# Rotary embedding of two cross attentions: a product on TensorE against elementwise work over two feature chunks

## The chip, the cores and the metric

One core of one Trainium2 chip runs the whole program. The metric is the device time of one execution in microseconds, the median of several runs.

## The reference, cut to what matters

The program is a decoder of two layers over 8 sequences of 512 tokens with 256 features. Each layer has a self attention, a cross attention and a feed-forward part. The change touches the two cross attentions. Both have 16 heads of 16 features, take queries from the normalised stream and keys and values from `ctx_1024` (8 x 512 x 256), and rotate pairs of features of queries and keys by an angle that depends on the token:

```python
# first cross attention: neighbouring features are a pair
x1, x2 = x[..., ::2], x[..., 1::2]
x1p, x2p = x1 * cos - x2 * sin, x1 * sin + x2 * cos
# second one: features d and d + 8 of a head are a pair
x1, x2 = x[..., :half], x[..., half:]
concatenate([x1 * cos - x2 * sin, x1 * sin + x2 * cos], -1)
```

Then come scores, softmax, the product with the values and an output product that is added to the stream. The first attends to all 512 tokens (with a mask of valid ones), the second to a window of 128.

## The kernel before, in words

The stages follow each other with a barrier between them: a banded attention, the first cross attention (`spread_attention`, L99), a feed-forward part, a self attention, the second cross attention (`window_attention`, L693), a mixture of experts. Within a cross attention a Python program writes out the order of the work of every engine by hand: the dictionary `at` gives each step a position in units, and each engine runs its own steps sorted by position. A unit is one pair of heads and a quarter of the tokens (32 units a batch, first stage) or half of them (16 units, second stage). For batch `b` the positions count from `o`, 32 `b` or 16 `b`, so the preparation of a batch (negative positions) falls among the units of the batch before. A step waits by semaphore for what it needs; an engine never passes a step that waits.

For each unit TensorE makes two products of scores. The "max" product (L347, L984) gives scores with queries on partitions, from which DVE takes row maxima (L522, L1186); it runs 13 or 8 units ahead. The "exact" product (L358, L1000) gives transposed scores less the maxima, which ACT exponentiates into `PT` (L456, L1112). In the second stage a product with a band of zeros and minus infinity (L971, "cover") comes ahead of each. The "value" products (L377, L1029) sum `PT` with the values. Scores use three slots of PSUM in the first stage, two in the second; all else goes through two or four banks `W`.

Scores are made at float32 precision from rounded parts: a row of the stacks `qs` and `ks` holds the high or low part of a feature, so that one product sums high*high, high*low and low*high. For two heads at a time 3 x 16 rows, a mask row (first stage) and two rows for the maxima stand in a half of 64 partitions: 49 and 51 rows, 48 and 50 in the second stage.

The preparation of a batch: DVE and POOL make the layer norm's mean and root ("stat", "root"), ACT normalises ("htok"), TensorE transposes ("norm"), and then for each of four projections (n = 1, 0, 3, 2: keys and queries of features 0 to 127, then of 128 to 255) there are

- "qk": two products on TensorE (L425, L1077), which ACT copies out of PSUM into `rows` (L485, L1146);
- "rot": a product with a permutation matrix (L433, L1085) that swaps the features of a pair; DVE multiplies its result by the signed sine, out of PSUM, into `rsin` (L554, L1225);
- "rope": on POOL, times the cosine (L617, L1291), plus `rsin` (L621, L1295), in the first stage and for queries times the mask (L629); ACT rounds this to the high part ("high", L491, L1153), and POOL subtracts that to get the low part (L636, L1301);
- "stack": SP copies the parts into the stacks, for each group of four heads and each of keys and queries in two times three DMAs of 64 KB (L308, L933), in the first stage with a mask row (L680). Four DMAs a group bring the maxima's rows (L313, L938).

For the first batch DVE does the whole rotation of the first queries, and every rotation runs before or beside the first maxima. The order of the projections lets group 0 be stacked once the first two are ready.

## Time and profile before

| | us |
|---|---|
| median of 3 runs | 3013.92 (3012.34 to 3017.20) |
| span of the profiled execution | 3008.1 |
| its own time | not recorded beside the span |
| first cross attention, from its first instruction to the next stage's | 263.3 to 844.1 |
| second cross attention, first to last | 2188.0 to about 2642 |

The profile is of one execution. Times in it count from the start of the span, which is the time from the first to the last instruction. PE is TensorE's matmul, PEld its weight load, DVE VectorE, ACT ScalarE, POOL GpSimd, SPq SyncE's DMA queue. The granted clock is the share of TensorE's full clock that it was given.

### The profile page before, as it was taken

Reading aid. Unit: us, or ns where it says so; the run is one execution under the profiler, and the core shown is the slowest. Engines: PE = TensorE matmul, PEld = TensorE weight load, DVE = VectorE, ACT = ScalarE, POOL = GpSimd, SP = SyncE. Lnnn points to the kernel's source line nnn. Section 1 sums busy time; section 2 is a strip of 40 time slices with the busy share of each in tenths; the row PEclk is TensorE's granted clock in tenths of the full one; section 3 lists DMA queues with packets and bytes.
Section 4 is the critical chain, followed back from the end, with each engine's and each line's share of the span. In section 5 each row is a group of like instructions: output and inputs, shape, how many; then the busy total and the mean of one; then the engine's idle time right before and its main releaser. Section 6 shows DMA issues by size and latency. Waiting matters only on the chain. (4 is left out here: it accounts for less than half of the span.)

```text
span 3008.1 us, 49289 instructions
## 1 busy us (share of the span) xinstructions
PE 2752.6 (92%) x16604; PEld 1616.4 (54%) x16605; DVE 1923.9 (64%) x3109; ACT 1450.5 (48%) x2231; POOL 1104.9 (37%) x853
## 2 busy tenths in 40 slices
PE   7997899999868899999999999999889999966998
PEld 4774333333335555555555555555445555556997
DVE  5775776667668766757575757575645555474565
ACT  3342566666668643434343434343335555553333
POOL 3233332222037243434343434443443333153333
PEclk9998899999989999999999999999989999958999
DMA  5002222222111000000000000000043222146665
GB/s 159 0 0 74 54 57 57 55 59 53 34 56 43 1 1 1 0 0 0 0 0 0 0 0 0 0 0 0 1 112 78 72 67 70 45 114 233 216 218 193
DMA packets 102929, 159.71 MB, mean 53 GB/s; under 512 B 28350, under 2 KB 63433, under 8 KB 97161
## 3 DMA queue, kind: packets, MB, share of 16 engines
q1 hardware_dynamic: 97784, 147.88, 17.1%
q0 software_dynamic: 3408, 8.46, 0.8%
q10 hardware_dynamic: 1600, 1.61, 0.2%
q8 instruction: 79, 1.29, 0.2%
q14 instruction: 58, 0.47, 0.1%
HBM read 91.79 MB, written 14.96 MB: 35 GB/s over the span
## 5 line engine op out<-in xcount | busy, mean ns | idle before, releaser
L1672 DVE TENSOR_REDUCE self_nmax<-self_SM 128x2 f32<-128x1024 f32 x256 | 313.9, 1226 | 184.5 <-PE self_SM L1569 177.7
L522 DVE TENSOR_REDUCE cross_nmax<-cross_S 128x2 f32<-128x1024 f32 x256 | 311.9, 1224 | 150.5 <-PE cross_S L347 149.6
L1650 ACT ACTIVATE self_PT<-self_ST 128x1024 f32<-128x1024 f32 x256 | 262.6, 1026 | 292.0 <-PE self_ST L1592 292.0
L1710 POOL TENSOR_TENSOR self_U<-self_PT 128x1024 f32<-128x1024 f32 x64 | 153.0, 2391 | 622.1 <-ACT self_PT L1650 622.1
L1713 POOL TENSOR_TENSOR self_U<-self_U,self_PT 128x1024 f32<-128x1024 f32 x128 | 304.0, 2375 | 55.6 <-ACT self_PT L1650 51.1
L456 ACT ACTIVATE cross_PT<-cross_S 128x1024 f32<-128x1024 f32 x256 | 260.9, 1026 | 114.6 <-PE cross_S L358 113.9
L1186 DVE TENSOR_REDUCE cross_nmax<-cross_S 128x4 f32<-128x1024 f32 x128 | 156.8, 1225 | 143.4 <-PE cross_S L984 143.3
L1602 PE MATMUL self_OP<-self_PT,self_V 128*64 128x512 f32 x1024 | 233.8, 598 | 10.1 <-ACT self_PT L1650 10.1
L1686 DVE RECIPROCAL self_rcp<-self_W 128x512 f32<-128x512 f32 x64 | 214.1, 3345 | 8.4 <-PE self_W L1609 8.4
L1112 ACT ACTIVATE cross_PT<-cross_S 128x1024 f32<-128x1024 f32 x128 | 131.1, 1024 | 119.6 <-PE cross_S L1000 119.6
L1602 PEld LDWEIGHTS self_OP<-self_PT,self_V 128*64 128x64 f32 x1024 | 69.5, 136 | 139.2 <-issue 132.8
L377 PE MATMUL cross_W<-cross_PT,cross_V 128*32 128x512 f32 x1024 | 135.7, 604 | 8.0 <-DVE cross_rsin L554 8.0
L617 POOL TENSOR_TENSOR cross_rows<-cross_rows,cross_cos 128x512 f32<-128x512 f32 x30 | 38.4, 1279 | 276.5 <-DVE cross_rsin L554 276.5
L358 PEld LDWEIGHTS cross_S<-cross_qs,cross_ks 51*128 51x128 f32 x512 | 47.9, 184 | 168.0 <-issue 120.9
L358 PE MATMUL cross_S<-cross_qs,cross_ks 51*128 51x512 f32 x512 | 128.1, 499 | 7.5 <-DVE cross_nmax L522 3.5
L1589 PE MATMUL self_ST<-self_q_hi,self_k_hi 64*128 64x512 f32 x512 | 122.9, 476 | 12.0 <-ACT self_PT L1650 10.8
L1654 ACT COPY self_Oraw<-self_OP 128x512 f32<-128x512 f32 x64 | 37.6, 588 | 197.2 <-PE self_OP L1602 197.2
L1569 PE MATMUL self_SM<-self_k_hi,self_q_hi 64*128 64x512 f32 x512 | 114.2, 441 | 19.1 <-DVE self_nmax L1672 19.1
L347 PE MATMUL cross_S<-cross_ks,cross_qs 49*128 49x512 f32 x512 | 108.6, 421 | 12.6 <-ACT cross_PT L456 11.4
L3103 PE MATMUL moe_TR<-moe_W,moe_hid_hi 128*128 x312 | 114.8, 406 | 0.0
L1617 PE MATMUL self_W<-self_wo,self_OT 128*128 128x256 f32 x512 | 112.5, 380 | 1.0 <-DVE self_OT L1689 1.0
L1689 DVE TENSOR_TENSOR self_OT<-self_Oraw,self_rcp 128x512 f32<-128x512 f32 x64 | 106.9, 1670 | 6.5
(436 smaller groups left out, 6335.7 us busy)
## 6 DMA issues: line engine op xcount, KB each, us to landing
moe_staged<-in_L_ffn_W SPq DMA_DIRECT2D x36, 1024.0 KB
cross_ks<-cross_parts SPq DMA_DIRECT2D x384, 64.0 KB, 2.2
cross_qs<-cross_parts SPq DMA_DIRECT2D x376, 64.0 KB, 2.3
all_x<-in_L_ffn_W SPq DMA_DIRECT2D x14, 1024.0 KB
all_x<-sorted_rows SPq DMA_DIRECT2D x83, 130.0 KB, 2.3
cross_cT<-in_ctx_T SPq DMA_DIRECT2D x16, 512.0 KB, 4.5
sorted_rows<-all_spare_row SPq DMA_DIRECT2D x1, 5460.0 KB, 23.8
all_x<-in_x SPq DMA_DIRECT2D x8, 512.0 KB, 3.7
```

The costliest lines, as they stand in the source:

```text
L358: m = pe.matmul(dst[:, r, :], ks[rows_r, p, k * P:(k + 1) * P], qs[rows_r, p, :], start=True, stop=True)
L377: m = pe.matmul(dst[32 * j:32 * j + 32, :], V[:, b % 2, k, 2 * p + r, :], PT[:, pt_slot[("exact", b, NT * p + k)], r, :], start=(k == 0), ...
L456: act.activation(PT[:, pt_slot[st], :, :], S[:, slot[st], :, :], ACT.Exp).then_inc(s_exped, 1)
L522: dve.tensor_reduce(nmax[:, g % 2, 0:R, n % PER_G], S[:, slot[st], :, :], AX.X, ALU.max, negate=True).then_inc(s_maxed, 1)
L1112: act.activation(PT[:, pt_slot[st], :, :], S[:, slot[st], :, :], ACT.Exp).then_inc(s_exped, 1)
L1186: dve.tensor_reduce(nmax[:, g % 2, 0:R, n0:n0 + 2], S[:, slot[st], :, :].rearrange("p r (i c) -> p r i c", i=2), AX.X, ALU.max, negate=Tru ...
L1602: m = pe.matmul(OP[j * D:(j + 1) * D, :], V[:, k, 2 * n + j, :], PT[:, k, j, :], start=(k == 0), stop=(k == NT - 1), skip_group_check=True)
L1650: act.activation(PT[:, k, :, :], ST[:, :, :], ACT.Exp).then_inc(exped.sem, 1)
L1672: dve.tensor_reduce(nmax[:, i, 0:P:D], SM[:, :, :], AX.X, ALU.max, negate=True).then_inc(maxed.sem, 1)
L1686: dve.reciprocal(rcp[:, :], bank_of(order, st)).then_inc(done, 1)
L1710: pool.tensor_tensor(U[:, c % 2, :, :], PT[:, 0, :, :], PT[:, 1, :, :], ALU.add).then_inc(added.sem, 1)
L1713: pool.tensor_tensor(U[:, c % 2, :, :], U[:, c % 2, :, :], PT[:, k, :, :], ALU.add).then_inc(added.sem, 1)
```

## The change

Each pair's two features now lie in different chunks of 128: one of each pair in features 0 to 127, its partner in the same row of the second chunk (the weights' columns and the biases are permuted on the host). The rotation then needs no product: with both chunks e = 0, 1 of keys (w = 1) or queries (w = 0) in `rows[:, e]`, DVE multiplies each by the sine ("sine"), POOL by the cosine, and POOL subtracts and adds the other chunk's sine product. ACT rounds both chunks, POOL makes both low parts. The "rot" steps are gone. The mask of queries is now a factor on the layer norm's `rstd`, on 4 columns, in place of a product on 512 and a cast for each batch.

A row of a stack is now 64 r + 8 d + 2 j + e (r head of the pair, d pair of features, j part, e chunk), so each DMA fills 16 rows in steps of eight, from 32 contiguous partitions of one part and chunk: six DMAs for keys and six for queries per group as before. The mask row is at 6, the maxima at 62 and 63, so the products use rows 0 to 61 and 0 to 63 of each half; the rows between are cleared once, `ks` by DVE and `qs` by POOL, at the start of each stage. Mask and maxima rows of both heads go in one DMA each (two and two a group in place of four and four).

`parts` holds keys and queries in two buffers of two chunks; a high part may only be written when all four groups of the batch before are stacked. `rows` and `rsin` are shared by keys and queries: `rows_freed` makes the eviction of queries wait for the whole rotation of keys. The first batch's queries use two slots of `PT` in their place. All positions of the preparation, of the value projections and of the first stage's output products are new.

```diff
-        for n, t in zip(QK_ORDER, (-44.0, -36.0, -28.0, -20.0)):
-            for part in range(KC):
-                at[("qk", b, n, part)] = o + t + part + 0.5
-            at[("rot", b, n)] = o + t + 2.9
-            at[("rope", b, n)] = o + t + 3.0
-            at[("high", b, n)] = o + t + 5.6
+        for w, t in ((1, -36.5), (0, -28.5)):
+            for e in range(2):
+                for part in range(KC):
+                    at[("qk", b, 2 * e + w, part)] = o + t + 2 * e + part
+        for w, t in ((1, -33.9), (0, -25.2)):
+            for e in range(2):
+                at[("sine", b, 2 * e + w)] = o + t + 2.0 * e
+            at[("rope", b, w)] = o + t + 2.2
+        for w, t in ((1, -28.0), (0, -21.0)):
+            for e in range(2):
+                at[("high", b, 2 * e + w)] = o + t + 0.1 * e
...
-        for m, ts in enumerate(((-14.4, -12.8), (1.6, 3.2))):
+        for m, ts in enumerate(((-20.5, -19.5), (-18.5, -17.5))):
...
-        for m, ts in enumerate(((41.6, 42.0), (43.2, 43.25))):
+        for m, ts in enumerate(((51.5, 52.5), (53.5, 54.5))):
...
+        def rows_freed(eng, b, w):
+
+            if (b, w) not in ((0, 0), (0, 1)):
+                roped(eng, *((b, 1) if w == 0 else (b - 1, 0) if b > 1 else (0, 1)))
...
-                elif kind == "rot":
-                    dst = free_bank(st)
-                    pe.wait_ge(s_act, nth_act[("qk", b, n, KC - 1)])
-                    if b == 0:
-                        pe.wait_ge(s_rot, 48)
-                    pe.matmul(dst, turnm[:, :], rows[:, n % 2, :], start=True, stop=True).then_inc(s_full, 1)
...
                 elif kind == "qk":
                     act.wait_ge(s_full, nth_full[st])
+                    rows_freed(act, b, n % 2)
+                    act.activation(rows_of(b, n % 2)[0][:, n // 2, :], src, ACT.Identity, scale=1.0 if n % 2 else scale).then_inc(s_act, 1)
                 elif kind == "high":
+                    w, e = n % 2, n // 2
+                    roped(act, b, w, LOW)
+                    if b and e == 0:
+                        for g in range(GROUPS):
                             stacked(act, b - 1, g)
+                    act.copy(parts[:, w, 0, e, :], rows_of(b, w)[0][:, e, :]).then_inc(s_high, 1)
...
+                elif kind == "sine":
...
+                    dve.wait_ge(s_act, nth_act[("qk", b, n, KC - 1)])
+                    dve.tensor_tensor(turned[:, e, :], row[:, e, :], sin[:, :], ALU.mult).then_inc(s_sine, 1)
...
+            pool.memset(qs[:, :, :].bitcast(F32), 0.0).then_inc(s_zero, 1)
...
+                    for e in range(2):
+                        pool.wait_ge(s_sine, nth_sine[("sine", b, 2 * e + n)])
+                        pool.tensor_tensor(rows[:, e, :], rows[:, e, :], cos[:, :], ALU.mult).then_inc(s_rope, 1)
+                    for e, op in enumerate((ALU.subtract, ALU.add)):
+                        pool.wait_ge(s_rope, base + 1 + e)
+                        pool.tensor_tensor(rows[:, e, :], rows[:, e, :], rsin[:, 1 - e, :], op).then_inc(s_rope, 1)
+                    for e in range(2):
+                        pool.wait_ge(s_high, nth_high[("high", b, 2 * e + n)])
+                        pool.wait_ge(s_rope, base + 3 + e)
+                        pool.tensor_tensor(parts[:, n, 1, e, :], rows[:, e, :], parts[:, n, 0, e, :].bitcast(F32), ALU.subtract).then_inc(s_rope, 1)
...
+                for e in range(2):
+                    eng.dma_start(stack[2 * j + e::STEP, pair, :].bitcast(F32), parts[from_, which, part, e, :].bitcast(F32)).then_inc(sem, 16)
```

The second stage has the same edits. Its new positions, for keys then queries:

```diff
+        at[("norm", b, 0)] = o - 22.2
+        at[("norm", b, 1)] = o - 20.2
+        for n, ts in ((1, (-19.5, -18.5)), (3, (-17.7, -16.7)), (0, (-15.6, -14.8)), (2, (-14.2, -13.4))):
+            for part, t in enumerate(ts):
+                at[("qk", b, n, part)] = o + t
+        for w, t in ((1, -17.9), (0, -13.9)):
+            at[("sine", b, w)] = o + t
+            at[("sine", b, 2 + w)] = o + t + (1.7 if w else 0.9)
+            at[("rope", b, w)] = o + t + (1.8 if w else 1.0)
+        for w, t in ((1, -14.9), (0, -11.6)):
+            for e in range(2):
+                at[("high", b, 2 * e + w)] = o + t + 0.05 * e
...
+        for m, t in enumerate((-10.5, -6.5)):
             for part in range(2):
+                at[("v", b, m, part)] = o + t + part
```

## Rows read from the trace of the kernel before

**Rows 1.** The page, part 1: busy time, share of span, instructions of each engine.

```profile
PE 2752.6 (92%) x16604; PEld 1616.4 (54%) x16605; DVE 1923.9 (64%) x3109; ACT 1450.5 (48%) x2231; POOL 1104.9 (37%) x853
```

**Rows 2.** Windows view: length, then PE, PEld, DVE, ACT, POOL busy, clock, DMA, GB/s.

```profile
262.00:289.50 27.50, 17.37 (x50) 9.15 (x50) 10.93 (x29) 9.90 (x18) 12.80 (x19) 0.88 0.55 156
289.50:313.20 23.70, 16.76 (x51) 6.16 (x50) 15.49 (x15) 4.18 (x8) 10.03 (x9) 0.78 0.42 94
313.20:831.00 517.80, 485.59 (x2726) 189.20 (x2726) 356.32 (x426) 334.05 (x433) 133.83 (x126) 0.99 0.21 52
...
2214.80:2237.00 22.20, 19.40 (x98) 8.38 (x94) 14.06 (x19) 3.69 (x7) 10.19 (x9) 0.77 0.44 107
2237.00:2627.00 390.00, 385.90 (x3684) 201.39 (x3684) 209.98 (x294) 216.78 (x305) 129.86 (x112) 1.00 0.27 67
```

**Rows 3.** Groups by line, whole span: busy us, mean ns | idle before, releasers.

```profile
L347 PE MATMUL cross_S<-cross_ks,cross_qs 49*128 49x512 f32 x512 | 108.6, 421 | 12.6 <-ACT cross_PT L456 11.4 <-DVE cross_nmax L522 0.5
...
L1592 PE MATMUL self_ST<-self_mrow,self_ones_r 64*128 64x512 f32 x512 | 102.0, 391 | 0.0
...
L617 POOL TENSOR_TENSOR cross_rows<-cross_rows,cross_cos 128x512 f32<-128x512 f32 x30 | 38.4, 1279 | 276.5 <-DVE cross_rsin L554 276.5
...
L433 PE MATMUL cross_W<-cross_rows,cross_turnm 128*128 128x512 f32 x64 | 35.8, 643 | 8.6 <-ACT cross_rows L485 5.1 <-issue 0.7
L1085 PE MATMUL cross_W<-cross_rows,cross_turnm 128*128 128x512 f32 x64 | 35.7, 641 | 4.2 <-ACT cross_rows L1146 2.4 <-issue 1.7
```

**Rows 4.** Waits from 313 to 831 us: us in total, times, longest us.

```profile
PE cross_S L347 <- ACT cross_PT L456: 11.4, 15, 3.3
...
PE cross_W L377 <- DVE cross_rsin L554: 8.0, 6, 1.3
```

**Rows 5.** Timeline of PE at a turn product: start us, us, instruction.

```profile
393.02 1.10 PE L433 MATMUL cross_W<-cross_rows,cross_turnm 128*128 128x512 f32 x2
394.05 0.51 PE L358 MATMUL cross_S<-cross_qs,cross_ks 51*128 51x512 f32 x2
```

**Rows 6.** Timeline of the start of the first cross attention, several engines.

```profile
263.40 1.80 POOL L587 MEMSET cross_V<- 128x2048 f32 x1
...
278.20 1.27 POOL L621 TENSOR_TENSOR cross_rows<-cross_parts,cross_rsin 128x512 f32<-128x512 f32 x1 [1.85 <-DVE cross_rsin L554]
...
278.76 1.26 DVE L563 TENSOR_TENSOR cross_rows<-cross_parts,cross_rsin 128x512 f32<-128x512 f32 x1
279.55 0.62 ACT L491 CAST cross_parts<-cross_rows 128x512 fp32r<-128x512 f32 x1 [2.90 <-POOLq L631]
...
286.33 3.73 SPq L308 DMA_DIRECT2D cross_ks<-cross_parts  x6
...
313.46 0.40 PE L358 MATMUL cross_S<-cross_qs,cross_ks 51*128 51x512 f32 x2
```

**Rows 7.** The page, part 6: DMA issues, KB each, median us to landing.

```profile
cross_qs<-cross_parts SPq DMA_DIRECT2D x376, 64.0 KB, 2.3
```

**Rows 8.** Timeline of PE, 321 to 325 us: a stall, idle time in brackets.

```profile
321.88 0.80 PE L347 MATMUL cross_S<-cross_ks,cross_qs 49*128 49x512 f32 x2 [3.28 <-ACT cross_PT L456]
...
324.32 2.07 PE L425 MATMUL cross_W<-cross_cT,cross_wk 128*128 128x512 f32 x2
```

**Rows 9.** Windows view of the stretch behind that stall, columns as in rows 2.

```profile
323.00:333.00 10.00, 10.00 (x30) 3.45 (x30) 5.23 (x6) 4.46 (x6) 0.00 (x0) 0.59 0.01 2
```

**Rows 10.** Timeline of PE, second cross attention: a unit, then a turn product.

```profile
2355.94 0.63 PE L971 MATMUL cross_S<-cross_band,all_ident_bf 64*64 64x512 bf16 x8
...
2357.52 1.12 PE L1085 MATMUL cross_W<-cross_rows,cross_turnm 128*128 128x512 f32 x2
2358.48 0.60 PE L1062 MATMUL cross_W<-all_ident,all_x 128*128 128x128 f32 x4
```

**Rows 11.** Timeline of DVE in the same stretch.

```profile
2357.28 1.23 DVE L1186 TENSOR_REDUCE cross_nmax<-cross_S 128x4 f32<-128x1024 f32 x1 [1.62 <-PE cross_S L984]
2358.68 0.69 DVE L1225 TENSOR_TENSOR cross_rsin<-cross_W,cross_sin 128x512 f32<-128x512 f32 x1 [0.18 <-PE cross_W L1085]
```

More of the change, by code:

```diff
@@ L796, in finishing @@
         return [st for st in steps if st[0] not in last_part or st[3] == last_part[st[0]]]
[L798 removed]
+    RINGED = ("norm", "qk", "v", "turn", "back", "out", "mt", "fix")
     BY_ACT = ("norm", "qk", "v", "back", "value")
[L800 removed]
+    ACT_DMA = [("stack", 0, 0, 2), ("mdma", 0, 0)]
     COVERS = ("cover_max", "cover_exact")
@@ L1234, in dve_program @@
-                    dve.tensor_tensor(row, low.bitcast(F32), rsin[:, n % 2, :], ALU.add).then_inc(s_early, 1)
-                    dve.wait_ge(s_early, 2)
-                    dve.wait_ge(s_high, nth_high[("high", b, n)])
-                    dve.wait_ge(s_early, ROPE - 1)
-                    dve.tensor_tensor(low, row, parts[:, n, 0, :].bitcast(F32), ALU.subtract).then_inc(s_early, 1)
+                    dve.wait_ge(s_sine, nth_sine[("sine", b, 2)])
+                    for e in range(2):
+                        dve.tensor_tensor(first_rows[:, e, :], first_rows[:, e, :], cos[:, :], ALU.mult).then_inc(s_early, 1)
```

511 lines of the change are left out of this document (219 added, 292 removed).

## The prediction, made before the changed kernel was run

> **What bounds the kernel now.** I read the busy shares first: TensorE is busy for 92% of the span, no other engine for more than 64% [rows 1]. An average over six stages settles nothing, so the windows view of the two cross attentions comes next [rows 2]. In the long middle of the second one TensorE is busy for 385.9 of 390.0 us at full clock: it is the bound, with nothing to spare. In the middle of the first it is busy for 485.6 of 517.8 us, so 32.2 us are idle; DVE, ACT and POOL are all far from full. At the starts the granted clock is 0.77 to 0.88, and TensorE waits for chains on other engines. The groups show what the change takes from TensorE: the turn products L433 and L1085, 32 in each stage (two records each) [rows 3]. The waits split the idle time of the first stage: 11.4 us for exponentials on ACT, 8.0 us for DVE to empty the bank of a turn product [rows 4].
>
> **The change, part by part.**
>
> *Turn products gone.* Busy sums of pipelined records say too much, so I take start to start: 393.02 to 394.05 is 1.03 us [rows 5]; in the second stage 2357.52 to 2358.48 is 0.96 us [rows 10]. 64 x 1.03 = **66 us** off the bound; the ends are 61 (0.96 each) and 71 (1.10, the row's own length). The bank waits go too: **8.0 us**.
>
> *Wider contraction.* The maxima's products go from 49 (48) rows to 62, the exact ones from 51 (50) to 64. Nearest row: 64 rows by 512 columns takes 391 ns, where 49 rows take 421 with their waits [rows 3]. Zero.
>
> *POOL* keeps six operations per pair of chunks at 1.28 us [rows 3] and loses the mask product. It is busy for 133.8 of 517.8 us [rows 2]; the cover is DVE's and ACT's lead, and only the order on ACT (below) exposes it. The added mask product on 4 columns per row group is as short and equally hidden.
>
> *DMAs.* Per batch SP issues 65 in place of 81 in the first stage, 57 in place of 65 in the second. Six issues take 3.73 us [rows 6] and one lands after 2.3 us [rows 7]. In the steady state SP is ahead; worth nothing there. The spread destination rows have no row here; same packets and bytes, so I take zero, with 1 us of landing either way, inside SP's lead.
>
> *A new hold on ACT.* This is the term that I trust least. Between exponentials 4 and 5 of a batch ACT now has: two copies to high parts of K, then the eviction of the first Q product, which by `rows_freed` must wait until POOL has written both low parts of K. From the first copy that is 0.62 + 1.28 + 1.28 and three hand-overs of 0.1 = 3.5 us [rows 3, 6], then 0.6 for the eviction. Behind it in ACT's queue stands the exponential; for it wait TensorE's third-next slot, and for the evicted bank the second Q product (only two banks). TensorE has about 1.9 us of other work in that time, so it stalls 2.2 us. The copies also wait for the stacks of the batch before: SP starts them at unit -1, 14 issues are 8.7 us and the landing 2.3, some 0.6 us later than ACT arrives. 2.8 us x 7 batches = **20 us lost**; ends 0 (ACT late anyway) and 58 (rival 1). In return the old ACT waits, **11.4 us**, go with the old order. One of them was dear: 3.28 us of idle [rows 8], after which a K product takes 2.07 us, and the granted clock is 0.59 over the next 10 us [rows 9], so **4 us** more come back. In the second stage the same hold falls into a unit with 3.6 us of other work and four banks: 0.2 us a batch.
>
> *Second stage, units left bare.* Today every unit has an extra product as filler. By the new times units 3 and 7 of 16 have none. A bare unit takes TensorE 1.58 us (2355.94 to 2357.52 [rows 10]), but its maxima must pass DVE first: from the second cover, 0.28 us into the unit at 2356.22, to the end of the reduction, 2357.28 + 1.23 = 2358.51 [rows 11], and some 0.1 for the hand-over is 2.4 us. Two such units give back 0.6 to 0.8 each; with the 0.2 above and a sine product that DVE may wait for ahead of a maximum, 1.7 us a batch, x 8 = **14 us lost** (0 to 24).
>
> *Starts.* Clearing `ks` on DVE and `qs` on POOL: 2048 elements took POOL 1.80 us [rows 6], so 4096 take 3.6. POOL's stands ahead of the layer norm's root, so Q is some 4 us later, and all four products and both rotations come ahead of the first stack. In the first stage the first maximum comes 3 us later, but the first exact product (313.46 now [rows 6]) waited on SP's chain and on ACT held by POOL; it comes near 306, with 7 us less work done ahead of it: even, 0. In the second the first exact product gains 4 us and 10 us of work is left for later: **6 us lost**. Ends: 5 gained, 15 lost.
>
> *DVE's sine product* now reads two SBUF operands; its old form read PSUM at 0.69 us [rows 11]. Alone 0.69 stays; beside POOL it may be 1.26 (rival 2). POOL waits for it, so they rarely meet: zero.
>
> Sum: 66 + 8 + 11.4 + 4 = 89.4 gained; 20 + 14 + 6 = 40 lost; net 49.4. The profiled execution spans 3008.1 us; no own time is given for it, so I set the runs' median 3013.92 beside it, 5.8 more, for what lies around. 3008.1 - 49.4 + 5.8 = 2964.5. **2964 us, 1.6% faster.**
>
> **Rivals.**
>
> 1. *The hold lowers the clock in the first stage.* For it: the idle of 3.28 us above was followed by half clock [rows 8, 9]; against: idles of 1.3 us [rows 4] were not (the middle holds 0.99 [rows 2]), and 2.8 lies between. An event costs 3.3 + 5 us (10 us of work at half clock); 7 x 8.3 = 58 in place of 20: 3002.
>
> 2. *Two SBUF operands beside POOL.* At 278.76 DVE's sum took 1.26 us, with POOL at work from 278.20, where its kind takes 0.69 alone [rows 6, 11]. If every one of 64 sine products does that, DVE loses 0.57 x 64 = 36 us; DVE is busy 54 to 69% [rows 2], so about half would reach the maxima: 18 lost, 2982. The Trainium skill, GPSIMD Engine Reference, section Specifications, says that GpSimd shares its SBUF interfaces with VectorE and contends with instructions that have two SBUF inputs; by that rule, which the 1.26 us bears out here, every sine product that meets POOL is dearer.
>
> 3. *Slower.* Place: the same hold on ACT, exponential 4 to 5 in the first stage and 1 to 2 in the second. Price: 8.3 us for each event with a fall of the clock, 14 events, 116 us. Then 89.4 - 116 - 6 - 14 = -47: 3060. It decides from (89.4 - 20) / 8.3 = 8.4, so from 9 of the 14 events. For: the second stage has two slots in place of three. Against: its unit there is long.
>
> 4. *TensorE's freed time is only idle.* If the chain DVE-POOL-ACT-SP per batch had the same length, 3014. Against: the middle of the second stage is 99% busy, with DVE and ACT at 54 to 56% [rows 2].
>
> **How the numbers follow.** Forecast 0.64 (its own range 2932 to 2986: turn products 61 to 71, the hold 0 to 30, bare units and starts at their ends); rival 1 0.12; rival 2 0.10; rival 3 0.08; rival 4 0.06. To hold 8 in 10 the range takes in rival 1: 2932 to 3005. A measurement can tell some 0.2%, 6 us. Faster: 0.64 + 0.10 + 0.10 of rival 1 = 0.84. Same: 0.02 of rival 1 and 0.06 = 0.08. Slower: 0.08.
>
> **What would show it.** No turn products; the middle of the second stage shorter by about 15 us, that of the first (to its last exact product) by 30 or more; TensorE idle for some 2.8 us once a batch in the first stage, with ACT's eviction of a Q product waiting for POOL; a first product of maxima 3 us later; bare units of 2.4 us. Wrong would be: a granted clock under 0.95 in either middle; sine products at 1.2 us throughout; maxima waiting for the stacks' DMAs; or exact products with 64 rows that are longer.

## The result, and the profile after

The changed kernel took 3020.5 us (median of 12 runs, 3016.8 to 3025.1), the kernel before 3013.8 on the same chip (12 runs): a ratio of 1.0017 with a 95% interval of 1.0009 to 1.0025. It is slower by 0.2% where 1.6% faster was forecast. The profiled executions stand further apart, 3008.1 and 3023.2 us (the changed kernel's is the slowest of its 12 runs, 3025.07 us), but they can be cut into stretches. Each row below is one execution; the cuts are first or last products of TensorE, except the start, which is the first instruction of the first cross attention (on POOL). "Middle" runs from the first exact product to the last, "max" is the first product of maxima, counted from the start of the stage (first) or from the end of TensorE's work in the self attention (second). Loads are the packets of the instruction queue q8.

| | start | max | middle | first cross | ffn + self | max | middle | second cross | rest | loads |
|---|---|---|---|---|---|---|---|---|---|---|
| before | 263.3 | 26.2 | 517.8 | 579.4 | 1344.2 | 28.0 | 390.4 | 452.8 | 368.5 | 79 |
| after | 265.3 | 31.3 | 503.0 | 565.3 | 1358.2 | 30.6 | 403.1 | 464.6 | 369.8 | 132 |
| difference | +2.0 | +5.1 | -14.8 | -14.1 | **+14.0** | +2.6 | +12.7 | **+11.8** | +1.3 | +53 |

So the first stage gained 14 us of the 36 that the steps of the prediction gave its middle, the second lost 12 where it should have gained, and 14 us went in two stages that the change does not touch. The cuts in the changed kernel, TensorE's timeline (start us, us, instruction):

```profile
817.41 0.50 PE L374 MATMUL cross_S<-cross_qs,cross_ks 64*128 64x512 f32 x2 [0.41 <-ACT cross_PT L466]
...
825.20 5.38 PE L418 MATMUL cross_W<-cross_wo,cross_OT 128*128 128x256 f32 x16 [0.77 <-ACT cross_OT L517]
839.31 0.56 PE L2254 MATMUL ffn_TP<-ffn_part,ffn_ones 128*128 128x1 f32 x2 [8.73 <-ACT ffn_sized L2337]
```

```profile
2177.73 11.06 PE L1595 MATMUL self_W<-self_wo,self_OT 128*128 128x256 f32 x50 [0.97 <-DVE self_OT L1667]
...
2219.34 0.80 PE L980 MATMUL cross_S<-cross_ks,cross_qs 62*128 62x256 f32 x4 [1.51 <-DMA cross_qs<-cross_parts]
```

The page of the changed kernel, busy time and instructions (as [rows 1]), and the instruction queue's line (packets, MB, share) of the kernel before and of the changed one:

```profile
PE 2722.1 (90%) x16461; PEld 1611.5 (53%) x16477; DVE 1937.8 (64%) x3116; ACT 1453.0 (48%) x2231; POOL 1085.0 (36%) x835
```

```profile
q8 instruction: 79, 1.29, 0.2%
```

```profile
q8 instruction: 132, 2.16, 0.3%
```

TensorE lost 30 us of busy time, of the 66 that were counted. Windows view of the changed kernel: the start of the first stage and both middles (columns as in [rows 2]).

```profile
289.50:313.20 23.70, 15.08 (x43) 6.40 (x44) 16.35 (x16) 5.24 (x10) 1.11 (x1) 0.57 0.48 125
314.40:817.40 503.00, 467.11 (x2674) 182.83 (x2672) 355.71 (x427) 339.10 (x436) 116.26 (x114) 0.96 0.22 54
2238.00:2641.20 403.20, 374.21 (x3634) 198.49 (x3636) 212.40 (x295) 216.29 (x306) 132.76 (x115) 0.97 0.26 65
```

Both middles hold a clock of 0.96 to 0.97, where they held 0.99 and 1.00 [rows 2]. The groups that answer to [rows 3] show no turn product, the wider products at nearly their old length (exact ones 508 ns against 499), and idle time in new places:

```profile
L374 PE MATMUL cross_S<-cross_qs,cross_ks 64*128 64x512 f32 x512 | 130.6, 508 | 3.7 <-DVE cross_nmax L531 3.2 <-ACT cross_PT L466 0.6
...
L363 PE MATMUL cross_S<-cross_ks,cross_qs 62*128 62x512 f32 x512 | 110.0, 427 | 18.5 <-DMA cross_qs<-cross_parts 9.1 <-ACT cross_PT L466 7.4 <-DVE cross_nmax L531 1.6
...
L965 PE MATMUL cross_S<-cross_band,all_ident_bf 64*64 64x512 bf16 x1024 | 88.4, 404 | 35.2 <-ACT cross_PT L1102 27.2 <-DVE cross_band L1198 7.3 <-DVE cross_nmax L1175 0.2
...
L441 PE MATMUL cross_W<-cross_hT,cross_wq 128*128 128x512 f32 x64 | 44.7, 795 | 17.9 <-ACT cross_rows L493 17.9
```

In the waits of the first middle the old row of 8.0 us for DVE [rows 4] is gone, and at the top stands TensorE in front of the second Q product. ACT's waits name who holds ACT, in both stages:

```profile
PE cross_W L441 <- ACT cross_rows L493: 17.9, 6, 3.6
PE cross_S L363 <- ACT cross_PT L466: 7.4, 11, 2.3
```

```profile
ACT cross_rows L493 <- POOL cross_parts L628: 15.0, 7, 2.1
...
ACT cross_parts L500 <- DMA cross_qs<-cross_qmask: 3.1, 6, 1.1
```

```profile
ACT cross_rows L1134 <- POOL cross_parts L1282: 15.1, 7, 2.2
...
ACT cross_parts L1142 <- DMA cross_qs<-cross_parts: 6.1, 4, 2.9
```

One such event in the first stage, all engines, in order of time:

```profile
652.02 1.14 ACT L500 CAST cross_parts<-cross_rows 128x512 fp32r<-128x512 f32 x2 [1.15 <-DMA cross_qs<-cross_qmask]
652.71 2.48 POOL L628 TENSOR_TENSOR cross_parts<-cross_rows,cross_parts 128x512 fp32r<-128x512 f32 x2 [4.03 <-ACT cross_parts L500]
...
655.29 0.60 ACT L493 ACTIVATE cross_rows<-cross_W 128x512 f32<-128x512 f32 x1 [2.14 <-POOL cross_parts L628]
...
655.94 2.08 PE L441 MATMUL cross_W<-cross_hT,cross_wq 128*128 128x512 f32 x2 [3.60 <-ACT cross_rows L493]
```

ACT makes the high parts of K at 652.02 (it had waited 1.15 us for the stacks of the batch before), POOL the low parts from 652.71 on, and only then, after 2.14 us, does ACT empty the bank of the first Q product. TensorE stood idle for 3.60 us in front of the second, and that product took 2.08 us where the same takes 1.12 at 2.4 GHz (at 647.91): it ran at 1.2 GHz (the granted clock is 0.50 from 654.8 to 661.5). This is the hold that the prediction described; it counted 2.8 us for it and no fall of the clock. In the second stage the same hold, which I had priced at 0.2 us a batch, is as long, and there ACT has work heaped up behind it. TensorE's wait in front of the covers, 27.2 us in the changed kernel, was this in the second middle of the kernel before:

```profile
PE cross_S L971 <- ACT cross_PT L1112: 3.6, 10, 0.5
```

One such event in the second stage:

```profile
2352.10 1.14 ACT L1142 CAST cross_parts<-cross_rows 128x512 fp32r<-128x512 f32 x2 [0.99 <-DMA cross_qs<-cross_parts]
...
2352.80 2.50 POOL L1282 TENSOR_TENSOR cross_parts<-cross_rows,cross_parts 128x512 fp32r<-128x512 f32 x2 [3.69 <-ACT cross_parts L1142]
...
2355.40 0.69 ACT L1134 ACTIVATE cross_rows<-cross_W,cross_bqs 128x512 f32<-128x512 f32 x1 [2.16 <-POOL cross_parts L1282]
...
2355.98 1.02 ACT L1102 ACTIVATE cross_PT<-cross_S 128x1024 f32<-128x1024 f32 x1
...
2357.35 0.71 ACT L1134 ACTIVATE cross_rows<-cross_W,cross_bqs 128x512 f32<-128x512 f32 x1
...
2358.40 2.10 ACT L1119 ACTIVATE all_x<-all_x,cross_shift,cross_rstd 128x256 f32<-128x256 f32 x4
...
2360.38 1.04 ACT L1102 ACTIVATE cross_PT<-cross_S 128x1024 f32<-128x1024 f32 x1
...
2361.47 1.06 PE L965 MATMUL cross_S<-cross_band,all_ident_bf 64*64 64x512 bf16 x8 [2.54 <-ACT cross_PT L1102]
```

From 2355.40 ACT does two evictions of Q, an exponential, two copies and the layer norm (2.10 us) before the next exponential at 2360.38; TensorE had been waiting 2.54 us for it, a unit behind a first stall of 1.21 us. The stall of 2.54 us falls into a unit that the new times leave bare; that unit takes 4.41 us in each of five batches.

### The profile page after: what moved, and what is told of

Its sections match the earlier page's. It is cut to its first block and busy times, and to the rows that moved or that the text cites. A ratio compares the mean times of both kernels' runs of the same rounds, so it can differ in the third digit from the quotient of the medians.

```text
span 3023.2 us, 48607 instructions
## 1 busy us (share of the span) xinstructions
PE 2722.1 (90%) x16461; PEld 1611.5 (53%) x16477; DVE 1937.8 (64%) x3116; ACT 1453.0 (48%) x2231; POOL 1085.0 (36%) x835
## 3 DMA queue, kind: packets, MB, share of 16 engines
q8 instruction: 132, 2.16, 0.3%
## 5 line engine op out<-in xcount | busy, mean ns | idle before, releaser
L374 PEld LDWEIGHTS cross_S<-cross_qs,cross_ks 64*128 64x128 f32 x512 | 48.7, 187 | 164.7 <-issue 133.9
L1567 PE MATMUL self_ST<-self_q_hi,self_k_hi 64*128 64x512 f32 x512 | 123.3, 478 | 12.7 <-ACT self_PT L1628 10.8
L374 PE MATMUL cross_S<-cross_qs,cross_ks 64*128 64x512 f32 x512 | 130.6, 508 | 3.7 <-DVE cross_nmax L531 3.2
L1632 ACT COPY self_Oraw<-self_OP 128x512 f32<-128x512 f32 x64 | 37.6, 587 | 197.4 <-PE self_OP L1580 197.4
L363 PE MATMUL cross_S<-cross_ks,cross_qs 62*128 62x512 f32 x512 | 110.0, 427 | 18.5 <-DMA cross_qs<-cross_parts 9.1
L965 PE MATMUL cross_S<-cross_band,all_ident_bf 64*64 64x512 bf16 x1024 | 88.4, 404 | 35.2 <-ACT cross_PT L1102 27.2
```

The source lines that it names most:

```text
L374: m = pe.matmul(dst[:, r, :], ks[rows_r, p, k * P:(k + 1) * P], qs[rows_r, p, :], start=True, stop=True)
```

## The experiments

All stretches, from the profiled execution of each kernel (columns as above):

| | median, us | first cross | ffn + self | second cross | loads |
|---|---|---|---|---|---|
| short_turn (before, products of one column) | 2998.9 | 578.3 | 1345.0 | 439.6 | 79 |
| pad_before, 98 waits | 3014.3 | 581.8 | 1345.2 | 451.3 | 80 |
| pad_before2, 140 waits | 3019.3 | 581.9 | 1346.0 | 452.4 | 80 |
| pad_before3, 196 waits | 3034.0 | 580.1 | 1362.4 | 450.1 | 134 |
| pad_after | 3012.1 | 567.8 | 1346.0 | 463.7 | 79 |
| clear_late | 3024.6 | 564.9 | 1359.0 | 463.3 | 132 |
| own_rows | 2983.4 | 534.6 | 1354.7 | 457.7 | 132 |
| all_four | 2977.5 | 536.5 | 1347.1 | 463.0 | 79 |
| htok_late | 2988.3 | 530.8 | 1358.4 | 461.5 | 132 |
| product_back | 3011.8 | 555.2 | 1345.0 | 474.7 | 79 |
| two_k_parts | 2974.1 | 531.3 | 1352.5 | 452.5 | 132 |
| first_only | 2972.0 | 531.5 | 1348.7 | 450.4 | 79 |
| tuned | 2963.9 | 532.3 | 1348.3 | 446.8 | 79 |

The start differs by as much (263.3 to 265.3) among kernels with the old code, so its shift of +2.0 us is not read. The kernel before took 3013.9 us beside own_rows, short_turn, pad_before and pad_after, 3016.7 beside clear_late, pad_before2, htok_late and all_four, 3015.1 beside pad_before3, product_back, two_k_parts and first_only, and 3013.1 beside tuned. Each stretch is of one execution. Equal code gives stretches that differ by 2.5 us in the first cross attention (by 3.8 with own rows, 530.8 to 534.6), by 2.7 in the second and by 4.5 in the long one; smaller differences are not read.

**The hold on ACT: own_rows.**

```diff
-        first_rows, first_sin = PT[:, PTS - 2, :, :], PT[:, PTS - 1, :, :]
+        first_rows, first_sin = s.sb("q_rows", [P, 2, T]), s.sb("q_rsin", [P, 2, T])
...
-            if (b, w) not in ((0, 0), (0, 1)):
-                roped(eng, *((b, 1) if w == 0 else (b - 1, 0) if b > 1 else (0, 1)))
+            if b:
+                roped(eng, b - 1, w)
...
-            return (first_rows, first_sin) if (b, w) == (0, 0) else (rows, rsin)
+            return (rows, rsin) if w else (first_rows, first_sin)
```

> The changed kernel, but queries have rows and sine products of their own in both stages, so the eviction of a Q product no longer waits for POOL's low parts of K. Theory A (the hold on ACT costs what the two middles lost): ACT's waits for POOL's parts, 15.0 us in the first stage and 15.1 in the second, vanish, and with them TensorE's 17.9 us before the second Q product, most of its 27.2 us before the covers, and the falls of the granted clock; first stage from 565 to about 540 us, second from 465 to about 443, in all about 2972. Rival B (the burst of copies, evictions and the layer norm on ACT, in that order, is too long by itself, or the high copies wait for the stacks of the batch before): TensorE idles nearly as long in front of the same products and the time falls by less than 12 us, to 3008 or more. The span of the self attention stays long (1358 us from the end of the first cross attention to the end of the self attention) in either.

Measured: 2983.4 us, a ratio of 0.990 (0.988 to 0.992) to the kernel before. The first stage went from 565.3 to 534.6, a little more than theory A gave; TensorE's wait in front of the second Q product fell from 17.9 to 5.3 us and the clock of the middle came back to 0.99. Waits of TensorE and windows view of own_rows, first middle:

```profile
PE cross_W L441 <- ACT cross_q_rows L493: 5.3, 6, 1.4
```

```profile
313.00:788.00 475.00, 454.13 (x2676) 179.63 (x2674) 355.52 (x428) 338.35 (x436) 116.32 (x114) 0.99 0.23 57
```

The idle time saved is 12.6 + 2.3 = 15 us. The other half of the 31 us is no idle time; a clock higher by 0.03 over some 500 us is worth 15 us and accounts for it. The second stage gained only 7 us of the 22 expected, and TensorE still waited 25.3 of the 27.2 us there for exponentials: in that stage theory A was wrong, and the hold is not what most of the idle time waited for.

**The place of the self attention's loop: pad_after, pad_before, pad_before2, pad_before3.** The self attention is the same code in both kernels. What was new there were stalls of a kind that the kernel before did not have, six times at the head of the loop, with no engine to wait for:

```profile
PE self_W L1514 <- issue: 8.1, 6, 1.7
```

```diff
             def _(pe):
                 pe_program(pe)
+                for _ in range(158):
+                    pe.wait_ge(s_full, 1)
```

> The changed kernel, with 158 semaphore waits that are met at once behind TensorE's last product of the first cross attention, so that every later instruction of TensorE stands at the place it had before the change. Theory C (the self attention's loop lies badly for the instruction loads since TensorE's code got shorter): instruction loads on TensorE's queue fall from 132 to about 80, the stretch from the end of the first cross attention to the end of the self attention from 1358 back to about 1344 us, in all about 3007. Rival D (those 14 us are of one execution, or come from something else, as the granted clock): 132 loads or a long stretch as before, about 3020 and a little more for the waits.

> The kernel before, with 98 semaphore waits behind TensorE's last product of the first cross attention, which moves its later instructions to the same place within a load of 256 instructions as in the changed kernel. Theory C: loads rise from 79 to about 132 and the stretch over feed-forward part and self attention from 1344 to about 1358 us; 3028 in all. Rival D: unchanged, 3014 to 3016.

pad_after: 79 loads, 1346.0 us for the stretch, 3012.1 in all (ratio 0.9985 to before). Theory C holds for it. pad_before did nothing, and neither did the next:

> The kernel before with 140 satisfied waits behind TensorE's last product of the first cross attention, in place of 98. If a wait is mostly no instruction of its own (the change then took 128 instructions from TensorE's code ahead of the loop, 64 matmuls with their weight loads, and not 158), this is the place of the changed kernel within 256, and loads rise from 79 to about 132 and the stretch over feed-forward part and self attention from 1344 to about 1357 us. If loads stay at 79 or 80, the place within 256 instructions is not what decides.

The reason was in the count of instructions on the page: 98 waits had added 50, 140 had added 71, since the builder joins two waits into one instruction. My condition had not been met by either. The last one doubles the number:

> The kernel before, with 196 satisfied waits behind TensorE's first cross attention. The builder joins two such waits into one instruction, so that 98 and 140 waits were 49 and 70 instructions; these are 98, and put the loop at the changed kernel's place within 256 instructions (158 fewer before the loop there). If that place decides: about 132 loads in place of 79 and 1357 us in place of 1344 for feed-forward part and self attention, in all some 3025. If it does not: 79 or 80 loads and 1344 to 1346 us.

It came out: 134 loads, 1362.4 us, 3034.0 in all, 0.57% slower (0.40 to 0.74%) than the kernel before by waits alone. Page of pad_before3, and its waits in the self attention:

```profile
q8 instruction: 134, 2.20, 0.3%
```

```profile
PE self_W L1538 <- issue: 8.1, 6, 1.5
```

So loads of 16.4 KB (2.16 MB in 132) are repeated in the loop or not, by where it lies. All the extra ones fall into the self attention: 12 packets on the instruction queue there in each of the nine kernels with 79 or 80 in all, 66 in each of the six with 132 or 134, so 54 more, nine for each of the six jumps back. The self attention alone, from its first product to its last, takes 1157.6 to 1159.3 us in the nine and 1166.3 to 1172.3 us in the six; in the changed kernel it is 1171.6 against 1159.2 before, and 11.6 of pad_before3's 18 us are there.

The change took 158 instructions from ahead of the loop (64 matmuls, 64 weight loads and 30 others, by the trace's count), and pad_after put 80 back: moved by -78, 0, +50 and +71 from its old place the loop is good, by +99 and by -158 bad. The last two differ by 257, which fits a period of 256; a rule without a period, by which a shift of more than some 80 either way is bad, would fit these runs as well. The Trainium skill, Runtime: NRT & Kernel Launch, section Instruction fetch mechanics, says that code comes in blocks of 16 KiB of 256 instructions, and that a taken branch to a place outside the two blocks of the current window stalls until it is fetched. The size of the loads agrees with that here, and so do the stalls at the loop's head (1.40 us of idle at 1330.17 in the changed kernel). The window of two does not: one turn of the loop is 1,584 instructions in the trace, over six blocks, and 12 loads for the whole stage leave none for the six jumps back.

**What a product's slot is worth: short_turn and product_back.** The first starts from the kernel before, cuts the turn product to one column and lets DVE read the rows; the swap of a pair's features is left out.

```diff
-   pe.matmul(dst, turnm[:, :], rows[:, n % 2, :], start=True, stop=True).then_inc(s_full, 1)
+   pe.matmul(dst[:, 0:1], turnm[:, :], rows[:, n % 2, 0:1], start=True, stop=True).then_inc(s_full, 1)
...
-   dve.tensor_tensor(rsin[:, n % 2, :], src, sin[:, :], ALU.mult).then_inc(s_dve, 1)
+   dve.tensor_tensor(rsin[:, n % 2, :], rows[:, n % 2, :], sin[:, :], ALU.mult).then_inc(s_dve, 1)
```

> The kernel before, with each turn product cut to one column of 512 and DVE's sine product reading the rows themselves: the swap of the pair's features is left out, all else, order and waits, stays. Theory E (the slots of the turn products are worth their length, as the prediction counted them): 64 times some 0.9 us less, about 2956, the middle of the second stage some 28 us shorter. Rival F (in the second stage DVE's and ACT's chain sets the unit, so that the freed time is idle): the second stage is shorter by less than 12 us, in all 2975 or more.

Measured: 2998.9 us (ratio 0.9952), 15 us for 64 products, where 58 were expected. In the second stage it is 13 us, 0.4 each. In the first it is 1 us, less than equal code differs by. Windows view of short_turn, first middle, second middle and one stretch:

```profile
313.00:830.00 517.00, 485.45 (x2734) 193.48 (x2734) 356.24 (x426) 335.59 (x435) 133.77 (x126) 0.96 0.21 52
2232.00:2612.00 380.00, 371.01 (x3670) 200.93 (x3666) 210.74 (x299) 213.69 (x303) 131.25 (x113) 1.00 0.28 69
723.00:733.00 10.00, 8.52 (x42) 2.98 (x40) 6.09 (x7) 5.13 (x6) 2.54 (x2) 0.74 0.20 48
```

In the first middle the clock is 0.96 where it was 0.99 [rows 2]: 0.03 of 517 us is 16 us at the full clock's pace, most of the 24 that shorter products should give (one takes 0.35 us where it took 1.10). The stall of 8.0 us for DVE [rows 4] is still there, in six waits of up to 1.33 us. The granted clock is 0.50 from 393.3 to 396.7, from 526.4 to 529.8 and from 659.5 to 666.3, each time at one of these waits; in the kernel before the same waits are as long and the clock does not fall at them. product_back starts from own_rows instead and adds work to TensorE alone:

```diff
+                    if kc == 0:
+                        pe.matmul(dst, w[:, kc, c * P:(c + 1) * P], src, start=True, stop=True)
                     m = pe.matmul(dst, w[:, kc, c * P:(c + 1) * P], src, start=(kc == 0), stop=(kc == KC - 1))
```

> The kernel with own rows for queries (2983 us), with the first of the two products of each Q and K projection made twice in both stages (the second one overwrites the first): 64 products more on TensorE, each of the size of a turn product, and no wait, no bank and no work on another engine more. The sum of the prediction counted such a product at 1.03 us. Theory K (once the holds are gone, TensorE's slot is worth its length in the first stage, 32 x 1.03 = 33 us, while in the second TensorE has idle time behind ACT, in which it hides): first stage from 535 to about 566 us, second from 458 to 462 to 470. Rival L (the slot is worth little in the first stage too, as the cut products of the kernel before suggest): first stage below 548.

First stage 555.2 (+20.6), second 474.7 (+17.0): 0.64 and 0.53 us a product (0.76 in the first stage against the fastest execution of equal code, 530.8). The first stage lies between both theories, the second above what either gave. In the first stage TensorE's 5.3 us in front of Q products were gone again, so part of the slot had been idle. The repeated products stand beside the projections and not where the turn products stood, so this prices a product of that size in the changed order. The extra 128 instructions ahead of the loop also moved it to -30 from its old place (79 loads), which is why the total rose by 28 us only.

**The start: clear_late.** In both stages:

```diff
-            pool.memset(qs[:, :, :].bitcast(F32), 0.0).then_inc(s_zero, 1)
...
                     pool.tensor_tensor(shift[:, :], shift[:, :], minus[:, :], ALU.mult).then_inc(s_root, 1)
+                    if b == 0:
+                        pool.memset(qs[:, :, :].bitcast(F32), 0.0).then_inc(s_zero, 1)
```

> The changed kernel, with POOL clearing the queries' stack behind the first layer norm's root instead of ahead of it, in both stages. Theory I (the clearing, 3.56 us, stands ahead of the root, and the whole start hangs on it): first product of maxima 3 to 4 us earlier in each stage (now 31.3 and 30.6 us from the start), in all 4 to 7 us less, about 3014. Rival J (all four projections and both rotations ahead of the first stack set the start, or the work left over moves elsewhere): the first maximum moves by less than 1.5 us or the first exact product does not move, in all 3018 to 3021.

The first maximum came 0.8 and 0.6 us earlier, no more than among kernels with equal code there (30.6 to 31.4 us in the first stage), and the total did not fall: rival J. POOL's timeline of clear_late shows what else stood there:

```profile
272.24 0.21 POOL L598 CAST cross_keep<-cross_m 128x32 f32<-128x32 uint8 x1 [4.29 <-DMA cross_m<-in_keep]
...
274.60 3.51 POOL L617 MEMSET cross_qs<- 128x4096 f32 x1
```

In the first stage POOL waits 4.29 us for the mask's DMA ahead of the root, and the clearing (3.56 us in the changed kernel) had been hidden in that wait. In the second stage there is no mask and ACT could begin to normalise earlier by 3.5 us, but TensorE was not ready for it: it waits for the context's DMA, and the first K products stand ahead of the transposes. TensorE's timeline of clear_late:

```profile
2196.49 3.75 PE L1074 MATMUL cross_W<-cross_cT,cross_wk 128*128 128x512 f32 x4 [6.91 <-DMA cross_cT<-in_ctx_T]
```

**The second stage: htok_late, two_k_parts, tuned.** In own_rows ACT waited there for POOL's root (6.4 us) in front of the layer norm, and for the stacks in front of the high parts of K (5.7 us). htok_late moves the normalisation from `o - 29.0` to `o - 25.5`.

> The kernel with rows of their own for queries (last experiment: 2983 us, second stage still 457.7 us with 25.3 us of idle TensorE before the covers), and in the second stage the layer norm's application on ACT put 3.5 units later. Theory G (ACT stands at the layer norm and waits for POOL's root, which is queued behind the low parts of K, and the exponential stands behind both; four waits, 6.4 us, each of which TensorE pays again with 2.1 us for the normalisation itself): ACT's wait for POOL's shift vanishes, TensorE's idle time before the covers falls from 25 to below 10 us, the second stage from 457.7 to about 442, in all about 2968. Rival H (ACT's burst and the wait of the high copies of K for the stacks are what counts): idle time stays above 18 us, second stage above 452.

Theory G fell, and rival H held: the wait for the root was gone, but another stood in its place, ACT's high parts waiting for POOL's rotation of Q, TensorE's idle time stayed at 25.0 us and the stage got longer by 4 us. ACT's waits in htok_late, second stage:

```profile
ACT cross_parts L1143 <- POOL cross_q_rows L1280: 14.3, 6, 5.3
...
ACT cross_parts L1143 <- DMA cross_qs<-cross_parts: 6.4, 4, 3.0
```

all_four put this edit together with own_rows, the late clearing and the 158 waits.

> Own rows for queries in both stages, the later normalisation in the second, the clearing behind the root in both, and 158 satisfied waits behind TensorE's first cross attention. If the four parts add up: 2983 (own rows) less 15 (normalisation), less 5 (clearing), less 8 to 12 (place of the loop), 2951 to 2957; loads 79. If the terms overlap (a later wait takes the place of a removed one), 2962 or more.

2977.5 us, not 2951 to 2957: of the four only own rows and the place of the loop gain anything. The late clearing does nothing that can be read, and with the late normalisation the second stage, 463.0 us, is as bad as in htok_late.

two_k_parts goes to the first late thing in that chain instead. `parts` gets a third buffer, and K uses two in turn:

```diff
+        def held(b, w):
+            return 2 * (b % 2) if w else 1
...
-                    if b and e == 0:
+                    if b >= 1 + w and e == 0:
                         for g in range(GROUPS):
-                            stacked(act, b - 1, g)
+                            stacked(act, b - 1 - w, g)
```

> The kernel with own rows for queries, and in the second stage parts of K in two buffers in turn, so that ACT's high copies of K no longer wait for the stacks of the batch before (5.7 us in four waits); queries share the sine products' buffer with keys, for want of room. Theory N (the first late thing in the second stage is that copy; POOL's low parts, its root of the layer norm and ACT's normalisation are late behind it, one after the other): TensorE's idle time before the covers falls from 25 to below 15 us, second stage from 458 to 448 or less, in all about 2973. Rival O (the burst on ACT between two exponentials, 2.1 us for the normalisation and 1.2 for two evictions, is long enough by itself): idle time stays above 18 us and the stage within 4 us of 458.

2974.1 us; ACT no longer waits for the stacks there, and for the root only once (2.3 us). TensorE's idle time before the covers went from 25.3 to 18.7 us and the second stage to 452.5. That is neither theory: the idle time is what rival O gave (above 18), the stage is shorter by 5 us, in theory N's direction and short of its numbers. What is left is mostly one stall per batch, 1.90 us, behind a burst on ACT. Timeline of two_k_parts:

```profile
2359.28 1.02 ACT L1107 ACTIVATE cross_PT<-cross_S 128x1024 f32<-128x1024 f32 x1 [1.07 <-PE cross_S L1001]
...
2360.93 0.69 ACT L1139 ACTIVATE cross_q_rows<-cross_W,cross_bqs 128x512 f32<-128x512 f32 x1
...
2361.63 1.28 POOL L1281 TENSOR_TENSOR cross_q_rows<-cross_q_rows,cross_cos 128x512 f32<-128x512 f32 x1
2361.65 1.81 DVE L1221 TENSOR_TENSOR cross_rsin<-cross_q_rows,cross_sin 128x512 f32<-128x512 f32 x1 [0.31 <-ACT cross_q_rows L1139]
...
2361.98 2.08 ACT L1124 ACTIVATE all_x<-all_x,cross_shift,cross_rstd 128x256 f32<-128x256 f32 x4
...
2363.96 1.00 ACT L1107 ACTIVATE cross_PT<-cross_S 128x1024 f32<-128x1024 f32 x1
...
2365.02 0.63 PE L970 MATMUL cross_S<-cross_band,all_ident_bf 64*64 64x512 bf16 x8 [1.90 <-ACT cross_PT L1107]
```

tuned adds to it the 158 waits and splits the normalisation (`o - 28.9` and `o - 27.9`, two images each), so that an exponential stands between the halves.

> Own rows for queries in both stages, two buffers for the parts of K in the second, 158 satisfied waits for the place of the loop, and in the second stage the normalisation on ACT in two halves with an exponential between them. Theory P (with the holds gone, what is left of the second stage's loss is the burst on ACT between two exponentials: 0.6 + 0.7 + 0.6 + 2.1 us, TensorE idle for 1.90 us once a batch, and the fall of the clock behind it): no idle of over 1 us left before the covers, second stage from 452.5 to 440 or less, in all 531 + 1347 + 440 and the rest: 2955 to 2960, loads 79. Rival Q (units without a filler product are as long as DVE's and ACT's chain, so that the second stage stays where it was before the change): second stage 448 to 453, in all 2965 to 2970.

2963.9 us, 1.65% faster than the kernel before (ratio 0.9835, 0.9821 to 0.9848), the best of all. The stall of 1.90 us is gone from every batch; one of 4.4 us at the start of the stage stayed, the others are under 1.0. The second stage is 446.8 us, between theory P (440) and rival Q (448 to 453), so neither is shown; the burst was worth some 6 us. Waits of TensorE in tuned, second stage, two rows of its timeline, and the group of Q's sine product on DVE:

```profile
PE cross_S L972 <- ACT cross_PT L1109: 11.8, 23, 4.4
PE cross_S L972 <- DVE cross_nmax L1182: 4.6, 6, 0.8
```

```profile
2461.51 0.41 PE L972 MATMUL cross_S<-cross_band,all_ident_bf 64*64 64x512 bf16 x4 [0.32 <-ACT cross_PT L1109]
2462.73 0.41 PE L972 MATMUL cross_S<-cross_band,all_ident_bf 64*64 64x512 bf16 x4 [0.80 <-DVE cross_nmax L1182]
```

```profile
L1223 DVE TENSOR_TENSOR cross_rsin<-cross_q_rows,cross_sin 128x512 f32<-128x512 f32 x16 | 18.5, 1169 | 6.1 <-ACT cross_V L1154 4.3 <-ACT cross_q_rows L1141 1.9
```

These rows name most of what is left besides the 4.4 us. A unit without any further product on TensorE takes 2.18 us from cover to cover, 0.31 of them idle for the exponential, twice a batch. And the 0.80 us for DVE stands once a batch behind a long sine product. With the hold gone, the sine product of Q's second chunk starts within 0.02 us of POOL's cosine product of the first, which the first sine product has released: it takes 1.81 us (as in the rows of two_k_parts above), the one of the first chunk 0.68. The mean of 1169 ns, where it was 688 before, mixes the two. That is rival 2 of the prediction, for one product in four; it costs DVE 16 x 0.48 = 8 us. In the changed kernel, where POOL's product had started 0.93 us earlier, the same product took 0.90 us.

**Part of the change alone: first_only.** The first stage of own_rows, the second one of the kernel before.

> Part of the change alone: the first cross attention as changed, with own rows for queries, the second as before, and 158 satisfied waits (79 instructions) behind TensorE's first cross attention. Theory M (the change pays in the first stage alone): first stage 535, feed-forward part and self attention 1346, second stage 452, in all about 2965, with 79 loads. Rival: the stages are not independent of each other (loads, clock), 2972 or more.

The median is 2972.0 us, which is the rival's number and not the 2965 of theory M. The profiled execution, the fastest of the four (2967.2 us), has its stretches and loads as theory M gave them (531.5, 1348.7, 450.4 and 79), and no stage shows an influence of the other; where the other 5 us of the median lie no trace shows. So the change pays in the first stage, and as it was made it loses in the second. The repaired second stage of tuned is shorter than the old code's by 3 to 6 us (446.8 against 450.1 to 452.8), little more than equal code differs by.

## Why the prediction was wrong, point by point

- *Turn products, 66 us*: **this step failed first, by its size.** It took the distance from start to start of a product for what its absence gives. Put back without any wait, a product costs 0.64 us in the first stage and 0.53 in the second: 37.6 for 64, and 28 of the 66 us were not there. In the kernel before, cutting them short gave 15 us, 1 in the first stage (the clock took it back) and 13 in the second. "TensorE busy for 99% of the middle" was a sum of modelled, overlapping records and did not say that every microsecond of it was needed.
- *Bank waits, 8.0, and old waits for ACT, 11.4*: the first are gone; in front of maxima 7.4 us for ACT remain, behind the new hold, and 5.1 without it.
- *The hold on ACT, 20 us*: the mechanism was right, place and length too (3.27 us from the first copy at 652.02 to the eviction at 655.29, 3.5 predicted; a stall of 3.60 us where 2.8 were taken). The size was not: removing it gave 31 us in the first stage, about half of it clock. This is rival 1, that the hold lowers the clock (priced at 58 us, 31 measured).
- *The hold in the second stage, 0.2 us a batch*: **this step failed.** ACT waited as long as in the first stage (15.1 us in seven waits against 15.0), and one eviction, two copies and the layer norm then stood between two exponentials. TensorE waited 27.2 us before covers, for which the sum had no term. The hold by itself was worth 7 of the 12 us that the stage lost; without it 25.3 us of the waiting stayed. A third buffer for the parts gave 5, and an exponential between the halves of the layer norm 6. So the missing term is the order of ACT's work: I had asked what other work TensorE has in that unit and not what ACT has still to do before the next exponential. Rival 3, slower through holds and falls of the clock in both stages, had the place; its 8.3 us an event was too dear (own_rows gave back 31 + 7 us for 14).
- *Bare units, 14 us lost*: about a third of it. A bare unit takes 2.18 us where 2.4 was forecast, with 0.31 us of idle time in place of 0.6 to 0.8: two of them in each of eight batches are 5 us. What ACT's burst adds in one of them is the term above.
- *Starts, 6 us lost*: the first maxima came 5.1 and 2.6 us later, the first exact products 1 us earlier in both. The first exact product of the first stage did not come near 306 (314.4), with the clock at 0.57 in the stretch before it and 9.1 us of waiting for the stacks' DMAs in front of the first maxima.
- *Zero for other stages*: **missing altogether**, 14.0 us in the profiled execution (12.4 of them in the self attention), and 8.4 of the medians by pad_after (3020.5 and 3012.1). No row of the kernel before showed it, and no step asked what the length of TensorE's code does to a loop behind it.
- *Wider contraction, POOL, DVE's sine product*: right. Exact products took 508 ns against 499; the sine product 681 ns on average in the first stage where it took 682, and 784 against 688 in the second, where the median is 693. Of rival 2 the changed kernel has little: five sine products of 0.90 to 0.91 us and one of 2.47, all in the second stage and beside POOL.
- *Rival 4, the freed time is only idle*: nearest by its number (3014), but only in part by its mechanism. TensorE's time was worth some 0.55 to 0.6 of its length (0.53 of 0.96 us, 0.64 of 1.03), not nothing.
- *Range and base*: the ends that the forecast names do not add up to its own range of 2932 to 2986; all good ends together give 2914, all bad ones 2998. The 3020.5 lies outside of both, and what put it there are the terms above. Of the 5.8 us added for what lies around the span some 4 belong to the difference between two executions: every other profiled run is 1.8 to 1.9 us longer than its span.

The sum with measured terms, profiled executions: first stage -14, second +12, loop +14, start and rest +3, together +15 us. The medians differ by 7. From the forecast's -49 to these +15 are 64 us; the turn products (28), the hold in the first stage (11 more than priced), the second stage's hold (7) and the loop (14) make 60 of them. That is an estimate from terms measured one by one on different kernels, not a closed account.

## What to carry to other kernels

A product on the busiest engine is worth what the trace gives when it is taken out or put in alone, not its own length; cut one to a single column, or repeat one, before counting a saving. Where a buffer is shared by two steps, look not only at the wait but at all that stands behind it in the waiting engine's queue up to the next instruction that the bound engine needs, and add the fall of the clock that followed such stalls here, which was worth about as much again as the idle time in the first stage. And read the stages that a change does not touch: a loop on an engine whose code got shorter or longer may fetch its instructions anew on every turn, and 158 satisfied waits, 80 instructions, ahead of it put it back here.

## What the runs showed of the hardware that I had not expected

- The place of a loop on TensorE: 12 loads or 66 in a stage whose loop turns seven times, and 1166.3 to 1172.3 us for that stage in place of 1157.6 to 1159.3, by a shift of +99 or -158 instructions of TensorE ahead of it.
- Freed work did not shorten the first stage: with the turn products cut to a column the first middle ran at a clock of 0.96 in place of 0.99 and was 1 us shorter, and the clock fell at waits of 1.33 us at which it had not fallen before.
- A product with two SBUF operands on DVE, beside a POOL instruction on 128x512 that had started before it, took longer than its 0.68 us by what that instruction had left, less some 0.13 us: 0.90 us with 0.35 left (changed kernel), 1.30 with 0.76 left (own_rows), 1.81 with 1.26 left (two_k_parts, tuned). It can be the other way round: at 2168.13 in two_k_parts DVE's second product follows its first without a break and takes 0.68 us, and POOL's instruction beside it takes 1.83 in place of 1.26. Beside POOL's instructions on four columns it stayed at 0.68 to 0.71.
